# A scan layer with gate and router: the gate moves to the finished sum, the scans get three PSUM banks, one bank serves all else

## The reference, cut to what matters

```python
resid_norm = resid * rsqrt(mean(resid * resid) + EPS) * norm_w
skip = resid_norm @ W_skip
x = silu(conv(resid_norm @ W_in) + conv_b)
delta = softplus(x @ W_delta_1 @ W_delta_2 + b_delta_2)
Bm, Cm, A = x @ W_B, x @ W_C, -exp(A_log)
h = h * exp(d_l * A) + (d_l * x_l) * B_l        # over l, for each channel and state
y_l = einsum('ben,bn->be', h, C_l)
out = resid + ((y + x * W_D) * silu(skip)) @ W_out
...
x = x + layernorm(out_of_layer);  x = x + layernorm(out_of_router(layernorm(x)))
```

## Time and profile before

| | us |
|---|---|
| median of three runs | 2529.62 |
| lowest, highest | 2523.74, 2530.01 |
| the profiled execution | 2525.85 |
| its span, first to last instruction | 2524.0 |
| first scan starts | 158.4 |
| last scan ends | 2388.6 |

### The profile page before, as it was taken

The page is one execution under the profiler, slowest core; times in us unless marked ns, Lnnn a source line. Parts: engine busy times, 40 slices in busy tenths (PEclk is TensorE's granted clock), DMA queues, the critical chain, the costliest instruction groups (busy, mean ns, idle before and its releaser), DMA issues. The chain is left out here.

```text
span 2524.0 us, 35818 instructions
## 1 busy us (share of the span) xinstructions
PE 1998.9 (79%) x11589; PEld 1601.8 (63%) x11589; DVE 1818.6 (72%) x3185; ACT 1861.0 (74%) x3716; POOL 1916.8 (76%) x1192
## 2 busy tenths in 40 slices
PE   4547676978888897888889797888879788788885
PEld 3446665757676675757677675758667575657552
DVE  3347776869687886968778786978768796777732
ACT  1467878697877878787878878787776978777631
POOL 0148887787878978788788978888787878899922
PEclk9878888989899998999989998999989899998996
DMA  3355556555465646556475655646465554646330
GB/s 124 101 170 161 171 164 199 190 175 192 141 220 166 212 143 199 179 166 214 127 238 181 190 161 173 216 155 205 143 213 173 166 175 147 210 156 190 117 108 17
DMA packets 239028, 425.94 MB, mean 169 GB/s; under 512 B 18878, under 2 KB 135162, under 8 KB 238842
## 3 DMA queue, kind: packets, MB, share of 16 engines
q1 hardware_dynamic: 238842, 423.65, 52.6%
HBM read 347.57 MB, written 76.02 MB: 168 GB/s over the span
## 5 line engine op out<-in xcount | busy, mean ns | idle before, releaser
L598 POOL TENSOR_TENSOR hc<-h,c_all 128x1024 f32<-128x1024 f32 x512 | 1206.2, 2363 | 326.1 <-PE y_sum L1185 285.6
L982 DVE TENSOR_TENSOR_SCAN h<-operand,carry,bank 128x512 f32<-128x512 f32 x480 | 592.9, 1270 | 177.2 <-PE bank L1180 107.2
L1180 PE MATMUL bank<-ident,u_t 128*128 128x128 f32 x2560 | 434.4, 297 | 304.2 <-DVE h L982 298.6
L1185 PE MATMUL y_sum<-ident,hc 128*128 128x128 f32 x4096 | 636.3, 288 | 14.0 <-POOL hc L598 13.2
L1180 PEld LDWEIGHTS bank<-ident,u_t 128*128 128x128 f32 x2560 | 316.4, 151 | 455.0 <-ACT u_t L708 214.3
L708 ACT ACTIVATE u_t<-dx_t,b_t 128x256 f32<-128x256 f32 x1280 | 578.5, 505 | 0.0
L1185 PEld LDWEIGHTS y_sum<-ident,hc 128*128 128x128 f32 x4096 | 521.6, 151 | 69.0 <-issue 42.1
L582 POOL TENSOR_TENSOR operand<-dx_q,b_all 128x1024 f32<-128x1024 f32 x192 | 453.7, 2363 | 32.1 <-DMA dx_q<-dx_dram 31.9
L982 DVE TENSOR_TENSOR_SCAN h<-bank,carry,operand 128x512 f32<-128x512 f32 x288 | 359.9, 1275 | 145.8 <-ACT bank L689 112.7
L689 ACT ACTIVATE operand<-delta_q,neg_a 128x512 f32<-128x512 f32 x640 | 435.8, 717 | 0.2
L689 ACT ACTIVATE bank<-delta_q,neg_a 128x512 f32<-128x512 f32 x384 | 264.0, 688 | 111.5 <-DVE h L982 109.9
(11 more groups left out here) (129 smaller groups left out, 2329.0 us busy)
## 6 DMA issues: line engine op xcount, KB each, us to landing
c_all<-bc_dram SPq DMA_DIRECT2D x256, 512.0 KB, 4.1
b_all<-bc_dram SPq DMA_DIRECT2D x192, 256.0 KB, 5.2
win<-in_L_attn_W_in SPq DMA_DIRECT2D x64, 512.0 KB, 5.1
wskip<-in_L_attn_W_skip SPq DMA_DIRECT2D x64, 512.0 KB, 5.0
xd_dram<-hv SPq DMA_DIRECT2D x64, 256.0 KB, 4.5
delta_dram<-delta SPq DMA_DIRECT2D x32, 512.0 KB, 4.2
dx_dram<-dx SPq DMA_DIRECT2D x32, 512.0 KB, 5.4
delta_q<-delta_dram SPq DMA_DIRECT2D x32, 512.0 KB, 5.3
```

Of the source, the lines that this page charges most:

```text
L598: nc.gpsimd.tensor_tensor(hc[:, s % 2], h[:, number % 3], c_all[:, j % 2, s % 2:s % 2 + 1].to_broadcast([P, 2, SPAN]), ALU.mult).then_inc( ...
L982: nc.vector.tensor_tensor_scan(h[:, number % 3, q], first, second, start, ALU.mult, ALU.add).then_inc(scan_done.sem, 1)
L1180: last = transpose(bank[:, q, b * P:(b + 1) * P], u_t[:, j % 2, b, q * P:(q + 1) * P], ident[:])
L1185: return matmul(to, lhsT=of, rhs=ident[:], is_transpose=True, start=start, stop=stop, skip_group_check=True)
```

## The change

The gate is applied where the quarter's sum leaves PSUM. The layout there is [position, channel], so the skip product is made in it too: `skip` multiplies the turned norm `rnt_s` (stored by `norm`, loaded once per stage) with `wskip`, half a product at a time, in slots 9, 12, 25 and 27; ScalarE's `tanh_skip` follows in the same slot, VectorE's `open_gate` one slot later, and `take_y`, now on VectorE, multiplies `y_sum` by the gate in slots 17 and 1. In `mix` ScalarE copies the turned sum to `ys` (slots 2, 3, 5, 7). The job `regate` goes, and with it the second load and norm. The output product accumulates in the two banks of the input product and is issued by halves of four tiles: `project_out` in slots 30, 31 (two) and 0. The additions to `z` stand in slots 0 and 1, the moments of `z` in slot 2, and the steps of `route` up to slot 11 two slots later. `bank` has three banks, taken in turn by (2 * number + q) % 3. `work[0]` and `work[3]` become one bank, `misc`; before each of its users TensorE waits for all earlier readers (`misc_free`).

```diff
+BANKS = 3
+KEPT = 6
...
-    ahead = {"norm": i + 3, "prep": i + 2, "scan": i, "regate": i - 1, "mix": i - 2, "route": i - 3}
-    return tuple(job for job, chunk in ahead.items() if 0 <= chunk < CHUNKS)
+    ahead = {"norm": i + 3, "prep": i + 2, "scan": i, "mix": i - 2, "route": i - 3}
+    jobs = tuple(job for job, chunk in ahead.items() if 0 <= chunk < CHUNKS)
+    return jobs + ("stage",) if "scan" in jobs and i % 2 == 0 else jobs
...
-            if s in (1, 4):
-                load_wskip(t, s // 3 + 2)
-            if s in (7, 10):
-                load_wskip(t + 1, s // 3 - 2)
+            if s == 14:
+                load_wskip(t + 1, 0)
+            if s == 29:
+                load_wskip(t + 1, 1)
+                if i % 2:
+                    load_rnt(t + 1)
...
-            if v := due(act, scan_done, t, 2 * (s - 1) + q + 1):
+            if v := due(act, scan_done, t, 2 * s + q + 1 - BANKS):
                 act.wait_ge(scan_done.sem, v)
-            to = bank[:, q]
+            to = bank[:, (2 * number + q) % BANKS]
...
-            if s == 1:
-                take_y(t - 1, 1)
-            if s == 17:
-                take_y(t, 0)
+            if s in (9, 12):
+                tanh_skip(t, 0, s // 12)
+            if s in (25, 27):
+                tanh_skip(t, 1, s // 27)
             if s == 30:
                 take_dxt(t + 1, 0, 0)
-            if s in (4, 7):
-                take_dxt(t, 1, s // 3 - 1)
-            if "regate" in jobs_now:
-                if s == 28:
-                    if v := due(act, xt_loaded, t, 1):
-                        act.wait_ge(xt_loaded.sem, v)
-                    if v := due(act, kept_moved, t, 1):
-                        act.wait_ge(kept_moved.sem, v)
-                    for b in range(TB):
-                        scaled(h2[:, b], h2[:, b], kept_now[:, 0, b:b + 1],
-                               kept_now[:, 1, b:b + 1]).then_inc(xt_normed.sem, 1)
-                if s in (30, 31):
-                    k = 2 * (s - 30)
-                    if v := due(act, xt_turned, t, k // 2 + 1):
-                        act.wait_ge(xt_turned.sem, v)
-                    if v := due(act, skip_done, t, PAIRS):
-                        act.wait_ge(skip_done.sem, v)
-                    for j in range(2):
-                        last = nc.scalar.activation(rnt_gate[:, k + j, :], work[3][:, j * T:(j + 1) * T],
-                                                    ACT.Copy, scale=nw[:, k + j:k + j + 1])
-                    last.then_inc(gate_rnt_ready.sem, 1)
+            if s in (4, 6):
+                take_dxt(t, 1, s // 6)
...
+                    if s == (2, 3, 5, 7)[p]:
+                        if v := due(act, y_turned, t, p + 1):
+                            act.wait_ge(y_turned.sem, v)
+                        if v := due(act, out_done, t - 1, TB):
+                            act.wait_ge(out_done.sem, v)
+                        nc.scalar.activation(ys[:, 2 * p:2 * p + 2, :].rearrange("p e t -> p (e t)"),
+                                             misc[:], ACT.Copy, scale=0.5).then_inc(ys_ready.sem, 1)
...
+    def open_gate(t, k, pair):
+        if not slot_of(t, 0):
+            return
+        if v := due(dve, thg_ready, t, 2 * k + pair + 1):
+            dve.wait_ge(thg_ready.sem, v)
+        if v := due(dve, y_read, t, 2 * k):
+            dve.wait_ge(y_read.sem, v)
+        nc.vector.scalar_tensor_tensor(
+            out=gate[:, 2 * pair:2 * pair + 2].rearrange("p b e -> p (b e)"),
+            in0=thg[:].rearrange("p b e -> p (b e)"), scalar=1.0, in1=misc[:], op0=ALU.add,
+            op1=ALU.mult).then_inc(gate_ready.sem, 1)
+    def take_y(t, k):
+        if not slot_of(t, 0):
+            return
+        if v := due(dve, hc_read, t, N * (k + 1)):
+            dve.wait_ge(hc_read.sem, v)
+        if v := due(dve, gate_ready, t, 2 * k + 2):
+            dve.wait_ge(gate_ready.sem, v)
+        if v := due(dve, y_stored, t, k):
+            dve.wait_ge(y_stored.sem, v)
+        for pair in range(2):
+            part = slice(2 * pair, 2 * pair + 2)
+            nc.vector.tensor_tensor(y_out[:, part], y_sum[:, part], gate[:, part],
+                                    ALU.mult).then_inc(y_read.sem, 1)
...
+            if s == 1:
+                take_y(t - 1, 1)
+            if s == 17:
+                take_y(t, 0)
+            if s in (10, 13):
+                open_gate(t, 0, s // 13)
+            if s in (26, 28):
+                open_gate(t, 1, s // 28)
+            if s in (0, 1) and t and "mix" in jobs[t - 1]:
+                if v := due(dve, out_done, t - 1, s + 1):
+                    dve.wait_ge(out_done.sem, v)
+                if v := due(dve, z0_ready, t - 1, TB):
                     dve.wait_ge(z0_ready.sem, v)
-                if v := due(dve, xt_normed, t - 1, TB):
-                    dve.wait_ge(xt_normed.sem, v)
-                if v := due(dve, s_ready, t - 4, 1):
-                    dve.wait_ge(s_ready.sem, v)
-                copied(kept_now[:], kept[:, (i - 1) % 4]).then_inc(kept_moved.sem, 1)
+                nc.vector.tensor_tensor(z[:, s], pair_bank(s)[:], z[:, s],
+                                        ALU.add).then_inc(z_ready.sem, 1)
...
+    def misc_free(t, ys=0, dxt=0, gates=0, h2t=0, w=0, wt=0, o=0):
+        for read, event in ((ys_ready, ys), (dxt_ready, dxt), (gate_ready, gates), (h2t_ready, h2t),
+                            (w_ready, w), (wt_ready, wt), (o_ready, o)):
+            if v := due(pe, read, t, event):
+                pe.wait_ge(read.sem, v)
...
+    def skip(t, k, pair, piece):
+        if not slot_of(t, 0):
+            return
+        if not piece:
+            misc_free(t, ys=PAIRS, dxt=4, gates=2 * k + pair, h2t=k * TB, w=k, wt=k, o=k * TB)
+            if v := due(pe, rnt_loaded, t - (FIRST + t) % 2, 1):
+                pe.wait_ge(rnt_loaded.sem, v)
+            if v := due(pe, wskip_loaded[k], t, 1):
+                pe.wait_ge(wskip_loaded[k].sem, v)
+        b = 2 * pair + piece
+        for d in range(KD):
+            last = matmul(misc[:, piece * QE:(piece + 1) * QE], rnt_s[:, d, b * P:(b + 1) * P],
+                          wskip[:, k, d, :], start=(d == 0), stop=(d == KD - 1))
+        if piece:
+            last.then_inc(skip_done.sem, 1)
+    def project_out(t, b, half):
+        if not (0 <= t < len(jobs) and "mix" in jobs[t]):
+            return
+        if not half:
+            if v := due(pe, ys_ready, t, PAIRS):
+                pe.wait_ge(ys_ready.sem, v)
+            if v := due(pe, rnt_ready, t, b + 1):
+                pe.wait_ge(rnt_ready.sem, v)
+            if v := due(pe, delta_ready, t, PAIRS):
+                pe.wait_ge(delta_ready.sem, v)
+            if v := due(pe, z_ready, t - 1, b + 1):
+                pe.wait_ge(z_ready.sem, v)
+        for et in range(half * HALF, (half + 1) * HALF):
+            last = matmul(pair_bank(b)[:], ys[:, et, b * P:(b + 1) * P], wout[:, et, :],
+                          start=(et == 0), stop=(et == ET - 1))
+        if half:
+            last.then_inc(out_done.sem, 1)
...
             turn_u(t, s + 1, 0)
             add_y(t, s - 2, 0)
+            if s in (9, 12):
+                skip(t, 0, s // 12, 0)
+            if s in (25, 27):
+                skip(t, 1, s // 27, 0)
             turn_u(t, s + 1, 1)
             add_y(t, s - 2, 1)
+            if s in (9, 12):
+                skip(t, 0, s // 12, 1)
+            if s in (25, 27):
+                skip(t, 1, s // 27, 1)
+            if s == 0:
+                project_out(t - 1, 1, 1)
...
+            if s in (30, 31):
+                project_out(t, 0, s - 30)
+            if s == 31:
+                project_out(t, 1, 0)
             if s == 30:
                 turn_dx(t + 1, 0, 0)
-            if s in (4, 7):
-                turn_dx(t, 1, s // 3 - 1)
+            if s in (4, 6):
+                turn_dx(t, 1, s // 6)
```

320 lines of the change are left out of this document (113 added, 207 removed).

## The result

The changed kernel takes 2742.97 us (median of 4 runs, 2740.73 to 2744.82) against 2529.82 (2523.74 to 2530.36): a ratio of 1.0849, 95% interval 1.0832 to 1.0865. It is 8.5% slower, where 2512 was forecast, and outside the range, which ended at 2585. The profiled execution took 2742.31 us.

The account below looks back on a forecast made before the run. No engine bounds everywhere: VectorE to slot 16, nobody in 17 to 24, ScalarE next, GpSimd at the turn. 4.4 + 2.6 - 5.9 = 1.1 a step, 13 over 12 steps, 16 with the end: 2512 us, range 2435 to 2585.

Parts of the forecast that it names:

- first stretch: Slots 2 to 16, bound by VectorE: its work falls, 61.60 us becomes 57.2, a gain of 4.4 a step.
- slots 17 to 28: ScalarE no longer waits in front of `y_out`, new waits take some back: 62.75 becomes 60.1, a gain of 2.6.
- the turn: Slot 28's weighing to scan 2: bunched output product costs 7.2 within a stage, 4.5 into a new one, together 5.9.
- the end: After the last scan: skip products go, output product lies behind the routing; 3 gained, between 10 gained and 5 lost.
- the sum: All terms of a step added: 4.4 + 2.6 - 5.9 = 1.1 us gained a step.
- Three banks: Transposes and exponentials can go one scan earlier, 1.27 us, removing waits only where TensorE had nothing else to do.
- The lower bound: First stretch: a gain of only 1 if ScalarE, reading `misc` in slots 2 to 7, holds up the convolutions.
- The prediction's own sign for this case: A first stretch as long as before would mean that ScalarE took VectorE's place there.
- The bound, "a loss of 5: Slots 17 to 28: worst case, both skip products held up once more for as long as their own length.
- The rival on the slower side: Slower by half clock or an in-order wait of the same size: 2560 to 2632, chance 0.35.
- Its first mechanism: Output product at 1.2 GHz in each turn: 48 us; 120 with 16 records and slot 25's skip product.
- Its second mechanism: An in-order wait of the same size as the half-clock loss, 48 to 120 us; shares the chance of 0.35.

Follow-up runs that it names:

- e2: The changed kernel with the first quarter's skip products one slot earlier on TensorE (slots 8 and 11), `thg` left in 9 and 12: 2680.3 us.
- e10: The changed kernel with the edits of e2, e3 and e8 together, plus ScalarE's copies into `ys` a slot later: 2564.8 us.
- e1: The changed kernel with two scan banks instead of three, the third left unused: 2886.7 us.
- e15: The moves of e13 with two scan banks, the freed bank taking the output product spread over slots 13 to 29: 2588.8 us.
- e3: The changed kernel with the second expert bias product (TensorE) and the second half of `o` (VectorE) one slot earlier: 2671.3 us.
- e13: e10 with both halves of the skip products of slots 25 and 27 in front of that slot's `u_t` transposes: 2515.3 us.
- e5: The changed kernel with 2 of the 8 matmuls of each output product left, all waits standing: 2625.9 us.
- e14: e13 with the first output product in slots 27 and 29, both norm transposes sharing the other pair bank: 2504.8 us.
- e16: e14 with the loads of `wskip` (second quarter) and `rnt_s` in slot 2 of the step using them: 2493.4 us, ratio 0.9856 to the kernel before.
- e8: The changed kernel with the second output product's halves one slot later (slots 0 and 1), its sum added into `z` in slot 2: 2725.7 us.
- e11: Against the changed kernel with e2, e3 and e8 together: skip products in 24 and 27, `thg` 25 and 28, gate 26 and 29, `o` 22 and 23: 2593.3 us.

## Why the prediction was wrong, point by point

A step was to take 1.1 less and took 14.1 more: 7.5 of the 15.2 between lie in the first stretch, 5.8 in slots 17 to 28, 1.9 in the turn. Over twelve steps that is 182 of the 231 us by which the forecast was off; 21 lie in the end, the rest in the four outer steps and the prologue, which were put at nothing. The step that failed is above all this: the sum has no term for ScalarE's wait in front of `thg` and `ys`, each in the same slot as the product that it reads. e2 measured 4.5 a step for the one and e10 3.5 for the other.

**Three banks: right in kind, far too small.** I priced the third bank at one scan, 1.27, let it count only where TensorE idled, and gave it no term in the sum. e1 measured 8.8 a step. The reading of it: where two banks make TensorE wait, the additions behind it are late, GpSimd's weighing behind them, and with it the scan two later, so that the wait is a link in a ring and not slack. e1 shows both waits growing together; that the 298.6 of the kernel before were such a link is argued, since no run gives that kernel a third bank. Since the bank helped more than forecast, the other terms were wrong by more than the total shows.

**First stretch: the wrong side of a bound that I had written down.** The lower bound, a gain of 1 "if ScalarE ... holds up the convolutions", was the right mechanism with no price of its own. It looked at the reads of `misc` in slots 2 to 7 alone; I did not ask what stands behind `thg` in slots 9 and 12, and took those two products from the gate's point of view, which waits 1.4. The prediction's own sign for this case, a first stretch as long as before, is what came. Priced from rows that I had, it was at hand: a skip product of 16 records takes 3.62, ScalarE is not the bound there and so arrives early and waits for all of it, twice. e2 measured 4.5 for `thg` and e10 3.5 for `ys`. Without both the stretch is 59.4, or 2.4 under the kernel before. How much of that is VectorE's relief and how much the third bank can't be told apart: with two banks and the same moves (e15) it is 67.0.

**Slots 17 to 28: half the gain, and a late product.** Measured from the end of scan 16 in the step shown: `low` was to begin 2.6 after it and begins 5.5 after it; the exponential of slot 25 was to be done after 29.8 and is done after 34.6 (39.3 before), so 4.7 of the 9.5 came, and scan 16 to 24 is 4.4 shorter. `o` was to be done after 34.5 and is done after 38.5. Then the half product took 3.78 and not 1.75, since it ran at 1.2 GHz behind the wait, and the two groups behind it 0.8 more. So GpSimd weighs slot 25 after 44.0, where 37.2 was forecast and 41.9 measured before. From there to the end of slot 28's weighing it is 21.9, near the 20.9 + 2 of the sum. The wait for `o` was foreseen; its date and the length of the product behind it were wrong. e3 took 5.3 of the stretch away, e13 another 3.5. The bound, "a loss of 5, if both are held up once more", was near the measured loss of 3.2 for the two stretches together; the value taken was a gain of 2.6.

**The turn: right in kind, 2 too small.** +7.8 against +5.9, and e5 puts 7.4 of it on the output product. The sign of the details too: VectorE waits for TensorE in front of `y_out`, 121.8 in all. Both kinds of turn were forecast too short, the one within a stage (25.9, measured 27.5) and the one into a new stage (26.9, measured 28.9). In the step shown the difference stands at the start: from slot 28's weighing to the first product the sum has 1.4, the trace 3.5, since the transposes of slot 30 wait for `u_t`:

```profile
1207.97 0.65 PE L1181 MATMUL bank<-ident,u_t 128*128 128x128 f32 x4 [1.83 <-ACT u_t L726]
...
1209.78 3.60 PE L1264 MATMUL pair_bank<-wout,ys 128*128 128x512 f32 x8
```

I gave 1 us in the turn into a new stage to the traffic of 1.5 MB; between e14 and e16, which takes the traffic away, those turns differ by 1.6.

**The end: wrong sign, 18 lost.** I set four skip products a step against an output product of 13.8 a step. As far as whole steps go that held: from one output product to the next it is 46.2 before (2414.55 to 2460.74) and 47.1 after (2636.01 to 2683.13). What I left out is that the last step's own turn has an output product as well, in front of `y_out`: 8.7 more from the last scan to `y_out`. The other 9 lie between `y_out` and the end and were not taken apart; the two blocks there take 16.59 and 15.25 and not 13.8, at granted clocks of 0.84 and 0.91. Before, the product lay beside the routing.

**The rival on the slower side** was given 0.35 and had the cause half right. Its first mechanism, the output product at the lower clock in every turn, did not come: the 16 records of slot 31 take 7.03, 0.44 each. The records that do run at 1.2 GHz are those of the skip products in slots 25 and 27, in slot 25 3.78 for eight behind a wait of 3.41; the rival had counted 1.8 a step for them, and it is 3.2. The page "TensorE: Matmul & The Clock Gate" of the Trainium skill, in its section on the clock gate, has the clock fall after little activity; the trace agrees in slot 25, and in the turn, where TensorE is busy 25.45 of 27.86, the granted clock stays at 1.00. Its second mechanism, an in-order wait of the same size, is what happened, 231 over the forecast where 48 to 120 were given.

**What stays open.** Of the 29 us of the outer steps and the prologue only the whole was measured. The turn into a new stage still costs 4 more than the others in e16, and 2.5 where both run at full clock (22.6 against 20.1); the round trip of `dx`, which is read as the cause of the wait in it, was not tried. How much of e3's gain is the order and how much the full clock that came with it can't be told apart by these runs.

## What to carry over

When an operation is put into a slot, price it on the engine that reads its result too: if the reader stands in the same slot, it arrives early, waits for the whole of it, and everything behind it in that queue is late. Putting the reader a slot later, or the producer earlier or in front of a wait that is there anyway, took no work away and was worth 228 us in five edits (e2, e3, e8, e10, e13). It is not free: e8 and e13 gave some back in the stretch behind, and e11 all of it, since `o` then stood in the same slot as the product that it reads. And a wait for a buffer that feeds back through three engines can be worth far more than the one instruction by which a third buffer lets it start earlier: it is measured with the buffer taken away, not argued from the idle time of one engine.

## What the chip showed that I had not expected

One more PSUM bank for the scans was worth 144 us, 5% of the time, though no engine was busy for over 79% of the span before. And mending the waits gave the clock back only in part: as a mean it is 0.886 in the changed kernel, 0.917 before, and 0.915 in e16. In the stretch from scan 24 to the weighing of slot 28 it rose from 0.77 to 0.89, while in the turn, where work was taken out and TensorE now waits, it fell from 0.99 to 0.89. In the last kernel the same work of TensorE in a turn takes 18.0 us or 21.9, and the turn 22.6 or 25.7.
